# Second parts of lookup tables: VectorE reads the raw values from PSUM copies that ScalarE makes

## The reference

```python
e = jnp.stack([tbl_0[ids[:, 0]], ..., tbl_25[ids[:, 25]]], axis=1)
combined = jnp.concatenate((dense_features[:, None, :], e), axis=1)
interactions = jnp.einsum('bfd,bgd->bfg', combined, combined)
iu, ju = jnp.triu_indices(27, k=1)
z = jnp.concatenate((dense_features, interactions[:, iu, ju]), axis=1)
h = jnp.concatenate([z, r_dense_features], axis=1)
h = jnp.maximum(h @ W_top1 + b_top1, 0.0)
h = jnp.maximum(h @ W_top2 + b_top2, 0.0)
y = h @ W_top3
```

## Time and profile before

| | |
|---|---|
| median of 3 runs | 380.93 us (380.3 to 381.95) |
| profiled execution, its time | 382.19 us |
| its span | 380.4 us |
| TensorE busy | 366.0 us, 96% |
| VectorE busy | 262.0 us, 69% |
| ScalarE busy | 233.4 us, 61% |
| GpSimd busy | 266.2 us, 70% |

### The profile page before, as it was taken

How to read it: one execution, slowest core, us unless ns; L and a number is a source line. 1 busy time by engine, 2 the same in 40 slices (tenths; PEclk the granted TensorE clock), 3 DMA queues, 4 the chain that set the end, 5 groups by cost and what they waited for, 6 DMA issues and landing times.

```text
span 380.4 us, 10834 instructions
## 1 busy us (share of the span) xinstructions
PE 366.0 (96%) x4408; PEld 349.1 (92%) x4408; DVE 262.0 (69%) x747; ACT 233.4 (61%) x480; POOL 266.2 (70%) x284
## 2 busy tenths in 40 slices
PE   8998688999999999999999999999999999999997
PEld 7887687999999999999999999999999999998897
DVE  5899857768597757949487775977579494933341
ACT  3486745658375656738556684756567385757572
POOL 6878777777777777777777777777777777777000
PEclk9999979999999999999999999999999999999999
DMA  8995353333333332433344332333333333212000
GB/s 179 253 256 183 109 142 91 86 83 87 75 90 81 91 83 66 101 81 81 81 90 89 76 92 76 88 84 84 85 73 97 87 74 84 56 52 59 7 4 0
DMA packets 25239, 34.77 MB, mean 91 GB/s; under 512 B 8522, under 2 KB 19042, under 8 KB 25190
## 3 DMA queue, kind: packets, MB, share of 16 engines
q0 software_dynamic: 8832, 18.11, 19.8%
q1 hardware_dynamic: 14278, 15.83, 16.3%
q10 hardware_dynamic: 2080, 0.15, 0.5%
HBM read 34.05 MB, written 0.01 MB: 90 GB/s over the span
## 4 chain that ended last, share of the span: by engine, by line
PE 77%; POOL 11%; issue 4%; ACT 3%; DVE 3%; DMA 1%; DVEq 0%
PE side L612 30%; PE prod L641 15%; POOL rows L345 11%; PE mlp L660 10%; PE side L623 8%; PE mlp L671 7%; PE mlp L662 3%; PE mlp L679 2%; ACT diag L391 2%; DVE onehot L490 1%; PE mlp L652 1%; DMA rows<-in_tbl,ids 1%; DVE table L504 1%; ACT feats L372 1%; PE prod L739 1%
## 5 line engine op out<-in xcount | busy, mean ns | idle before, releaser
L345 POOL DMA_INDIRECT rows<-in_tbl,ids x276 | 265.3, 961 | 84.9 <-issue 81.4
L490 DVE TENSOR_SCALAR onehot<-wanted,row_no 125x256 fp32r<-125x256 int32 (+1 forms) x554 | 172.7, 384 | 13.8 <-PE side L612 7.6
L391 ACT ACTIVATE diag<-prod 32x216 f32<-32x216 f32 x256 | 87.6, 342 | 96.8 <-PE prod L641 77.3
L612 PE MATMUL side<-onehot,table_hi 125*128 125x256 f32 x556 | 142.1, 294 | 0.9 <-issue 0.5
L612 PE MATMUL side<-onehot,table_lo 125*128 125x256 f32 x556 | 136.9, 284 | 0.0
L612 PEld LDWEIGHTS side<-onehot,table_hi 125*128 125x128 f32 x556 | 107.1, 193 | 2.2 <-issue 1.6
L612 PEld LDWEIGHTS side<-onehot,table_lo 125*128 125x128 f32 x556 | 107.4, 193 | 0.0
L518 DVE TENSOR_SCALAR h<-mlp,b_sb 128x128 f32<-128x128 f32 x86 | 24.9, 346 | 90.5 <-PE mlp L662 54.2
L372 ACT ACTIVATE feats<-side 128x512 f32<-128x512 f32 (+2 forms) x80 | 79.3, 1035 | 4.1 <-PE side L623 2.9
L641 PE MATMUL prod<-feats 128*64 128x54 f32 x2048 | 73.0, 223 | 1.9 <-ACT feats L372 1.9
L641 PEld LDWEIGHTS prod<-feats 128*64 128x64 f32 x2048 | 64.8, 138 | 10.2 <-ACT feats L372 2.5
(11 more groups left out here) (57 smaller groups left out, 147.8 us busy)
## 6 DMA issues: line engine op xcount, KB each, us to landing
wanted<-in_small_ids SPq DMA_DIRECT2D x62, 128.0 KB
rows<-in_tbl,ids POOLq DMA_INDIRECT x276
feats<-in_tbl SPq DMA_DIRECT2D x7, 448.0 KB
dense<-in_dense_rows SPq DMA_DIRECT2D x16, 64.0 KB
w_sb<-in_w_pairs SPq DMA_DIRECT2D x1, 702.0 KB
table<-in_tbl SPq DMA_DIRECT2D x1, 560.0 KB
w_sb<-in_tbl SPq DMA_DIRECT2D x1, 560.0 KB
w_sb<-in_w SPq DMA_DIRECT2D x1, 512.0 KB
```

Of the source, the lines that this page charges most:

```text
L345: gp.indirect_dma_start(rows[:, q % SLOTS_OF_ROWS, f * D:(f + 1) * D], None, large_tables[g + f], bass.IndirectOffsetOnAxis(ap=ids[:, t, g ...
L391: last = nc.scalar.activation(diag[t % 2][part, s * SEG_GROUPS * SLOTS:(s + 1) * SEG_GROUPS * SLOTS] .rearrange("p (g r) -> p g r", g=SEG_ ...
L490: made = nc.vector.tensor_scalar(onehot[v % 2][:, c - row_nos_at(h), :], wants, row_no[:, c:c + 1], None, ALU.is_equal)
L612: last = nc.tensor.matmul(look_bank(v)[:, 0:BS], part_of(part, k)[:, c * D:(c + 1) * D], onehot[v % 2][:, c, :], start=(c == 0 and part is ...
```

## The change

ScalarE copies each raw table, in pieces of up to 512 columns, into one of three PSUM banks that are free then (`mlp` and the second banks of `prod[0]` and `prod[1]`), and VectorE subtracts from there, a piece at a time. There are 20 pieces: 0, 1 (table 1); 2, 3 (table 3); 4, 5 (table 5); 6, 7, 8 (table 7); 9, 10 (table 0); 11, 12 (table 2); 13, 14 (table 4); 15, 16 (table 6); 17, 18, 19 (table 8). The counters `raw_staged` and `lo_made` take the place of `lo_ready`. `stage(j)` from j = 3 on waits for VectorE to have made piece j - 3. VectorE's `second_part(8)` moves behind the clearing of the padding, and stages 17, 18, 19 lie in segments (0, 0), (0, 1), (0, 2) of ScalarE's loop, each behind that segment's `empty_turn`.

```diff
+PIECES = tuple((k, a, min(a + BANK, CH[k] * D)) for k in (1, 3, 5, 7, 0, 2, 4, 6, 8) for a in range(0, CH[k] * D, BANK))
+PIECES_OF = tuple(tuple(j for j, piece in enumerate(PIECES) if piece[0] == k) for k in range(NT))
+STAGES = 3
...
+        def stage_bank(j):
+            a, b = PIECES[j][1:]
+            return (mlp, prod[0][:, BANK:], prod[1][:, BANK:])[j % STAGES][0:CP, 0:b - a]
...
-            sp.wait_ge(lo_ready[NS], 1)
+            sp.wait_ge(lo_made, PIECES_OF[NS][-1] + 1)
...
+            def stage(j):
+                if j >= STAGES:
+                    act.wait_ge(lo_made, j - STAGES + 1)
+                elif j:
+                    act.wait_ge(first_wanted_ready, 4 * j)
+                k, a, b = PIECES[j]
+                nc.scalar.activation(stage_bank(j), raw_table(k)[:, a:b], ACT.Copy).then_inc(raw_staged, 1)
...
                 if v == NS:
-                    for k in range(NS):
-                        act.wait_ge(lo_ready[k], 1)
+                    act.wait_ge(lo_made, PIECES_OF[NS - 2][-1] + 1)
...
             round_table(1)
+            stage(0)
+            stage(1)
...
             for v in range(6, NS):
                 copy_first_ids(v)
+            stage(2)
             empty_lookup(1)
+            stage(3)
...
             round_table(5)
+            stage(4)
             empty_lookup(3)
+            stage(5)
...
             round_table(7)
+            stage(6)
             empty_lookup(5)
+            stage(7)
+            stage(8)
...
             empty_lookup(6)
+            stage(9)
             empty_turn(0, 3)
+            stage(10)
             round_table(4)
             empty_lookup(7)
+            stage(11)
             empty_turn(0, 4)
+            stage(12)
             round_table(6)
+            for j in range(13, 17):
+                stage(j)
             round_table(NS)
...
                         if s == 1:
                             place_dense(t + 1)
+                    if t == 0 and s < 3:
+                        stage(17 + s)
                     for v in lookups_at(t, s):
                         empty_lookup(v)
...
             def second_part(k):
                 dve.wait_ge(hi_ready[k], 1)
-                nc.vector.tensor_tensor(part_of(table_lo, k), raw_table(k), part_of(table_hi, k).bitcast(F32),
-                                        ALU.subtract).then_inc(lo_ready[k], 1)
+                for j in PIECES_OF[k]:
+                    dve.wait_ge(raw_staged, j + 1)
+                    nc.vector.tensor_tensor(piece_of(table_lo, k, j), stage_bank(j),
+                                            piece_of(table_hi, k, j).bitcast(F32), ALU.subtract).then_inc(lo_made, 1)
...
             second_part(6)
-            second_part(NS)
-            for k in range(NS):
-                dve.wait_ge(lo_ready[k], 1)
+            dve.wait_ge(lo_made, PIECES_OF[NS - 2][-1] + 1)
             dve.wait_ge(look_full, NS)
             for i in range(2, FEAT_TILES):
                 clear_pads(i)
+            second_part(NS)
...
                     pe.wait_ge(hi_ready[k], 1)
-                    pe.wait_ge(lo_ready[k], 1)
+                    pe.wait_ge(lo_made, PIECES_OF[k][-1] + 1)
```

More of the change, by code:

```diff
@@ L196, in tower_program @@
         hi_ready = [sem(f"hi_ready{i}") for i in range(NT)]
-        lo_ready = [sem(f"lo_ready{i}") for i in range(NT)]
+        raw_staged = sem("raw_staged")
+        lo_made = sem("lo_made")
         onehot_ready = sem("onehot_ready")
@@ L251, in part_of, with piece_of @@
             return part[:, CH_AT[k] * D:(CH_AT[k] + CH[k]) * D]
+        def stage_bank(j):
+            a, b = PIECES[j][1:]
+            return (mlp, prod[0][:, BANK:], prod[1][:, BANK:])[j % STAGES][0:CP, 0:b - a]
+        def piece_of(tables, k, j):
+            a, b = PIECES[j][1:]
+            return tables[:, CH_AT[k] * D + a:CH_AT[k] * D + b]
         def row_nos_at(h):
```

## The result

The changed kernel takes 390.08 us, median of 5 runs (388.87 to 390.68), the kernel before 380.68 us (380.26 to 381.95, 5 runs). The ratio is 1.0239, with a 95% interval of 1.022 to 1.0258: slower, as forecast, but by 9.4 us where 5.6 were forecast, and outside the stated range, which ended at 389.0. The profiled execution has a time of 388.87 us and a span of 387.1, against 382.19 and 380.4 before: 6.7 us more.

A forecast was written before the change was run, and what follows sets the result against it. The loop runs at TensorE's pace, so start-up losses reach the end: lookup 12 at 65.6 against 60.0 gives +5.6 us, 382.19 to 387.8, less 1.26 for the median, 386.5 us; range 383.6 to 389.0.

The forecast's parts named there:

- The stretched gathers and what they are worth: GpSimd, 9.9 to 44.3 us: VectorE's subtractions stretch gathers by 4.0 us; TensorE's 4.43 us wait could be won back.
- ScalarE's added copies: ScalarE's 20 copies to PSUM: 0.50 us in the queue per 512 columns, together 9.5 us.
- VectorE's pieces: VectorE's subtractions from PSUM: 0.67 us per 512 columns, 0.13 of it fixed, bounds 0.60 and 0.80.
- The piece 10 wait: VectorE before one-hot 9: piece 10 waits for stage 10 on ScalarE, which comes some 0.8 us late.
- Up to one-hot 9: VectorE through tables 7, 0 and 2: 0.7 us more plus a late stage 10; one-hot 9 ends at about 41.1.
- The new wait of stage 16: ScalarE: stage 16 waits for piece 13 until 41.9, so lookup 9 starts at 46.15; TensorE idles 4.1 us.
- The aside: TensorE before lookup 9: with one-hot 9 at 39.63, turn (1, 0)'s copy still ends at 44.4, losing 3.2 us.
- The second chain: One-hot 10 waits behind table 8's last piece, stage 19 and turn (1, 2); lookup 10 starts at 56.3.
- SyncE's queue: Lookup 11's ids queue behind the pair weights, sent at 53.95; one-hot 11 starts at 59.5, lookup 11 at 61.9.
- The low clock: TensorE at 1.2 GHz after idles, at about 45 to 50 and 55 to 60 us; lookup 9 takes 3.4 us.
- the sum: Lookup 12 at 65.6 against 60.0, so +5.6 us, carried to the end of the profiled execution: 387.8.
- The fast rival: Freed GpSimd decides: gather 30 lands at 43.0, the 4.43 us wait goes; -4.6 us, 376.3; chance 0.07.

The follow-up runs named there:

- sbuf: Changed kernel with copies to PSUM and waits kept, but VectorE's pieces read the raw table in SBUF; 389.41 us, 1.0220 times the kernel before.
- order_only2: Kernel before, no copies to PSUM, one-hots 10 and 11 ahead of table 8's second part, pair weights later; 383.68 us, 1.0085 times the kernel before.
- wlate: Kernel before with only the pair weights loaded later, behind the ids of lookup 15; 383.53 us, 1.0064 times the kernel before.
- stage16b: Changed kernel with only stage 16 moved behind the copy of turn (1, 0); 387.51 us, 1.0174 times the kernel before.
- oh_ids2: Changed kernel with one-hot 10 ahead of table 8's second part and lookup 11's ids ahead of the pair weights; 385.26 us, 1.0128 times the kernel before.
- onehot10b: Changed kernel with only one-hot 10 made ahead of the second part of table 8; 391.39 us, 1.0250 times the kernel before.
- again2: Changed kernel without any edit, timed and profiled again; 389.25 us, 1.0205 times the kernel before.
- awake: Changed kernel with 32 extra matmuls on TensorE while it waits for one-hot 10; 389.16 us, 1.0217 times the kernel before.
- all4: Changed kernel with stage 16 behind turn (1, 0)'s copy, one-hots 10, 11 before table 8's second part, weights behind lookup 15's ids; 379.81 us, 0.9960 times before.

## Why the prediction was right in kind and wrong in size

Point by point:

- *The stretched gathers and what they are worth.* Right. They vanish, and with the chains in place they buy nothing (sbuf). The prediction took the 4.43 us of waiting for GpSimd's lateness; most of it was the pair weights (order_only2 and wlate).
- *ScalarE's added copies*, 0.50 us in the queue: 0.52 (9.88 to 10.40), some more behind a copy from `side`.
- *VectorE's pieces*, 0.67 us by a surcharge of 0.13 for PSUM: wrong, 0.61 (10.56 to 11.17). In sbuf the pieces take 681 ns from SBUF, as long as the 0.68 to 0.69 from PSUM. The piece 10 wait, 0.8 us: 0.83.
- *Up to one-hot 9*, end at 41.1: 41.8, with 0.87 us from the slow first lookup of this execution.
- *The new wait of stage 16*, at 41.9: 42.45. Lookup 9 at 46.15: 46.80; idle 4.1: 3.64. stage16b shows that this wait is the cause of 2.4 us of the 5.6 by which lookup 9 is late. The aside that 3.2 us are lost even without VectorE's lateness is 0.2 us low by its own terms: 46.1 less 1.5 is 44.6 and not 44.4.
- *The second chain*, lookup 10 at 56.3: 57.32.
- *SyncE's queue*, one-hot 11 at 59.5: 60.63. Lookup 12 at 65.6: 67.14. oh_ids2 against onehot10b shows that the two waits stand in series.
- *The low clock*: two stretches, as forecast, though the first came later than given (48 to 51; the second 55 to 61). Lookup 9 and products (0, 2) together took 4.55 us (46.80 to 51.35), as the sum had it, and that is luck: the sum had the whole lookup at the low clock and the products at the full one, and in the trace it was the end of the lookup and the products.

**The step that failed** is the sentence "It lies 1.26 us above the median of 380.93, so the forecast is 386.5 us". It carried the offset of one execution of the old kernel over to the median of the new, which has no reason to share it. Measured, the profiled execution of the changed kernel lay not 1.26 us above its median but 1.21 below (388.87 against 390.08): that is 2.5 of the 3.6 us by which the forecast missed. The other 1.1 us is the sum, +5.6 where the two profiled executions are 6.68 apart; 0.87 of it is the first lookup, which differs by execution. Put together, the difference of the medians is 6.68, plus 1.51 by which the old kernel's profiled execution lay above its median (382.19 against 380.68), plus 1.21: 9.40. Against again2 it was 8.2 us, so the size itself is uncertain by about 1 us.

What makes the two offsets stays open. The clock goes with them: the three executions of the old kernel with a mean clock of 0.991 took 381.81, 382.19 and 382.37 us, against medians of 380.7 to 381.0, and the changed kernel took 387.68 to 389.89 at 0.987 and 389.24 to 390.68 at 0.982. But the traces don't make the low stretches the whole cause. In the trace of before, the low stretch is followed by 0.89 us in which TensorE waits for the rows of a gather begun at 55.72, which no work of TensorE held up; a faster lookup 10 would only have lengthened that wait. In the changed kernel the second low stretch is hidden (awake), and the sum had both stretches in it anyway. The first one costs something: in again2, at 0.982, all of lookup 9 is slow (3.74 us against 2.66), and lookup 12 starts at 67.63 in place of 67.14. That is 0.5 us of the 1.21. An execution of the old kernel near its median wasn't traced.

The fast rival was rightly kept small: its condition, stage 16 not holding up ScalarE and one-hot 10 ready in time, is what all4 makes true, and it is ahead then, but by 0.4% and not 1.2%.

## What to carry to other kernels

A copy that is counted at 0.5 us on an engine with gaps can cost five times that (2.4 us for stage 16), if its wait stands ahead of work that a third engine needs: follow each new wait to what is queued behind it, then to what that releases, until the chain ends. Waits in series hide each other, so an edit that removes one of them can show nothing, or even a loss where it moves a low clock out of another wait's shadow; try them together before giving up the idea. And a sum made against one profiled execution shouldn't be shifted to a median by that execution's offset, unless it is known what the offset is made of and that the change leaves it alone.

## What the runs showed of the hardware

A subtraction of 125 x 512 float32 took 0.68 us on VectorE whether the raw operand lay in SBUF (sbuf) or in PSUM (the changed kernel). TensorE began its first lookup at about half rate while the granted clock was recorded as 1.00, and left that rate at a time that varied: in the changed kernel two matmuls started per 0.4 us until 10.8 us and three to four after, before it was three to four from 8.8 us on, and over the traces the same 16 matmuls from 8.43 us on took 3.8 to 5.2 us. With whole tables of 1024 and 1280 columns the second SBUF operand cost GpSimd 4.0 us (before), in pieces of 512 only 1.7 (sbuf), one trace each. The 702 KB of pair weights, sent while rows were on their way, put the landing of gather 30's rows off by 3.25 us (before against order_only2).
